# Five extra matmuls into an unread PSUM bank ahead of the first matmul of the feed-forward's context expert

## The reference, cut to what matters

```python
x = x + _layernorm(_L0_attn_ref(_layernorm(x), ...))   # long convolution along the tokens
x = x + _layernorm(_L0_ffn_ref(_layernorm(x), ...))    # 8 routed experts + a shared one
x = x + _layernorm(_L1_attn_ref(_layernorm(x), ...))   # 16 heads, causal, 2 null keys
x = x + _layernorm(_L1_ffn_ref(_layernorm(x), ...))    # 4 unlike experts, top 2 of 4
```

```python
logits = x @ router_w + router_b + load_balancer
e0 = silu(x @ sw_w1) * (x @ sw_w3) @ sw_w2
syn = x @ ce_syn_w + ce_syn_b
attn = (syn @ ce_wv + ce_bv) @ ce_wo + ce_bo
h2 = _layer_norm(syn + attn, ce_n1g, ce_n1b)           # the context expert, e2
```

## Time and profile before

| | us |
|---|---|
| median of 3 runs | 1162.09 |
| lowest, highest | 1157.04, 1163.64 |
| the profiled execution, its own time | 1157.97 |
| its span, first to last instruction | 1156.2 |
| mean granted TensorE clock | 0.962 |

### The profile page before, as it was taken

One profiled execution on the slowest core, in us unless ns is written; L12 is line 12 of the kernel. 1 busy time (PEld: TensorE's weight loads), 2 busy tenths in 40 slices (PEclk: granted clock), 3 DMA queues, 4 the chain that ended last, 5 costly groups with the idle time before them and its releaser, 6 DMA issues.

```text
span 1156.2 us, 18943 instructions
## 1 busy us (share of the span) xinstructions
PE 1017.6 (88%) x6783; PEld 832.9 (72%) x6783; DVE 797.4 (69%) x2569; ACT 561.1 (49%) x1075; POOL 582.1 (50%) x561
## 2 busy tenths in 40 slices
PE   0568799899988999899998999899999999899976
PEld 0446688578965889568886789668886788669844
DVE  7676666868488666887578685886678764883464
ACT  4217542764346542673436633565427743485421
POOL 4226463754537462655627644574627643565422
PEclk9967899999999999999999999999999999999988
DMA  6200000000000000000000000000000000000000
GB/s 153 70 1 1 10 1 1 1 10 2 1 10 1 10 1 10 1 10 1 1 10 1 10 1 1 10 10 1 1 10 1 1 1 10 1 1 2 10 1 9
DMA packets 21853, 11.29 MB, mean 10 GB/s; under 512 B 7424, under 2 KB 21120, under 8 KB 21632
## 3 DMA queue, kind: packets, MB, share of 16 engines
q1 hardware_dynamic: 18048, 8.84, 2.9%
q10 hardware_dynamic: 3712, 1.25, 0.4%
HBM read 7.99 MB, written 2.10 MB: 9 GB/s over the span
## 4 chain that ended last, share of the span: by engine, by line
PE 47%; DVE 31%; POOL 8%; ACT 6%; issue 6%; DMA 0%; SPq 0%; DVEq 0%; POOLq 0%; ACTq 0%
PE bank L1757 9%; PE bank L1533 6%; POOL rnorm L783 4%; PE bank L1759 4%; ACT square L965 3%; PE bank L1657 3%; PE bank L1717 3%; PE bank L1526 3%; PE bank L1829 3%; PE bank L1527 3%; PE bank L1528 3%; DVE x4m L1494 2%; DVE sumsq L1371 2%; PE bank L1787 2%; PE bank L1723 2%
## 5 line engine op out<-in xcount | busy, mean ns | idle before, releaser
L783 POOL TENSOR_TENSOR rnorm<-sumsq,minus_half 128x16 f32<-128x16 f32 x64 | 192.9, 3027 | 27.0 <-DVE sumsq L1374 27.0
L791 POOL TENSOR_TENSOR square<-square,causal 128x256 f32<-128x256 f32 x128 | 91.6, 747 | 100.4 <-ACT square L1003 100.4
L791 POOL TENSOR_TENSOR unit<-unit,causal 128x256 f32<-128x256 f32 x128 | 90.3, 737 | 85.9 <-ACT unit L1003 85.9
L1398 DVE TENSOR_TENSOR denom<-bank,null_sum 128x4 f32<-128x4 f32 x128 | 20.4, 159 | 122.3 <-PE bank L1759 122.2
L1717 PE MATMUL bank<-qT,kT 64*128 64x256 f32 x512 | 96.4, 389 | 0.0
L1371 DVE TENSOR_REDUCE sumsq<-square 128x16 f32<-128x1024 f32 x64 | 77.9, 1217 | 14.5 <-ACT square L965 14.4
L1757 PE MATMUL bank<-val,unit 128*128 128x128 f32 x512 | 82.2, 283 | 4.2 <-DVE mixed L1402 4.2
L958 ACT ACTIVATE unit<-bank 128x512 f32<-128x512 f32 x128 | 72.1, 599 | 28.0 <-PE bank L1528 24.9
L1380 DVE TENSOR_TENSOR unit<-unit,rnorm 128x1024 f32<-128x1024 f32 x64 | 79.0, 1241 | 8.9 <-POOL rnorm L783 7.6
L1757 PE MATMUL bank<-val,square 128*128 128x128 f32 x512 | 82.3, 283 | 2.6 <-DVE mixed L1402 2.6
L1723 PE MATMUL bank<-qT,kT 64*128 64x128 f32 x512 | 84.0, 284 | 0.5 <-ACT unit L1003 0.3
(11 more groups left out here) (360 smaller groups left out, 2782.3 us busy)
## 6 DMA issues: line engine op xcount, KB each, us to landing
out<-x SPq DMA_DIRECT2D x8, 256.0 KB, 2.2
xin<-in_L_attn_x SPq DMA_DIRECT2D x7, 256.0 KB, 2.7
square<-in_L_attn_w_kv SPq DMA_DIRECT2D x1, 1024.0 KB, 7.8
w_sw<-in_L_ffn_sw_w SPq DMA_DIRECT2D x3, 256.0 KB, 8.2
unit<-in_L_attn_w_q SPq DMA_DIRECT2D x1, 512.0 KB, 6.4
w_out<-in_L_attn_w_out SPq DMA_DIRECT2D x1, 512.0 KB, 4.3
w_ml<-in_L_ffn_ml_w SPq DMA_DIRECT2D x2, 256.0 KB, 5.7
xin<-in_L_attn_x ACTq DMA_DIRECT2D x1, 256.0 KB, 3.0
```

The lines of the kernel that those rows point to most:

```text
L783: pool.tensor_tensor(rnorm[:, k, t, :], sumsq[:, t % 2, k, :], minus_half[:], ALU.pow).then_inc(a_root.sem, 1)
L791: m = pool.tensor_tensor(pd, pd, causal[:].unsqueeze(1).to_broadcast([P, 2, P]), ALU.mult)
```

## The change

A new step `f_warm` is played on TensorE. It waits for nothing, and it signals nothing. It issues five matmuls of one fp32r weight slice with 512 columns of the same tile, `w_kv.hi`, into bank 6. `f_ce.0` overwrites part of bank 6 later, and nothing reads what `f_warm` wrote. The step is in three of the tables, so in seven rounds.

```diff
 MIDDLE = { "PE": """
-a_m.0 a_m.1 a_null f_turn.0 f_turn.1 f_ce.0 f_ce.1 f_sw.0 ...
+a_m.0 a_m.1 a_null f_turn.0 f_turn.1 f_warm f_ce.0 f_ce.1 f_sw.0 ...
 LAST_L = { "PE": """
-a_m.0 a_m.1 f_turn.0 f_turn.1 a_null f_ce.0 f_ce.1 f_sw.0 ...
+a_m.0 a_m.1 f_turn.0 f_turn.1 a_null f_warm f_ce.0 f_ce.1 f_sw.0 ...
 LAST_A = { "PE": """
-a_m.0 a_m.1 f_turn.0 f_turn.1 a_null f_ce.0 f_ce.1 f_sw.0 ...
+a_m.0 a_m.1 f_turn.0 f_turn.1 a_null f_warm f_ce.0 f_ce.1 f_sw.0 ...
...
+            def f_warm(g):
+
+                for _ in range(5):
+                    mm(bank[6][:], w_kv.hi[:, 0:P], w_kv.hi[:, 0:N], start=True, stop=True)
...
-                "f_turn": f_turn, "f_ce": f_ce_, "f_sw": f_sw, ...
+                "f_turn": f_turn, "f_warm": f_warm, "f_ce": f_ce_, "f_sw": f_sw, ...
```

More of the change, by code:

```diff
@@ L82 @@
     "PE": """
-a_m.0 a_m.1 a_null f_turn.0 f_turn.1 f_ce.0 f_ce.1 f_sw.0 f_me.0 l_turn2 a_t.0 f_ceT f_sw.1 a_m.2 f_sw.2 f_relu.0 a_v.0 f_relu.1 a_t.1
+a_m.0 a_m.1 a_null f_turn.0 f_turn.1 f_warm f_ce.0 f_ce.1 f_sw.0 f_me.0 l_turn2 a_t.0 f_ceT f_sw.1 a_m.2 f_sw.2 f_relu.0 a_v.0 f_relu.1 a_t.1
 f_ce2 a_m.3 f_sw.3 f_me.1 a_v.1 f_ml.0 f_ml.1 f_ce2T a_t.2 f_ml.2 f_ml.3 a_t.3 l_turn3 a_v.2 a_v.3 l_route f_out.0
@@ L112 @@
     "PE": """
-a_m.0 a_m.1 f_turn.0 f_turn.1 a_null f_ce.0 f_ce.1 f_sw.0 f_me.0 a_t.0 f_sw.1 f_ceT a_m.2 f_relu.0 f_relu.1 a_v.0 f_sw.2 f_ce2 l_turn2
+a_m.0 a_m.1 f_turn.0 f_turn.1 a_null f_warm f_ce.0 f_ce.1 f_sw.0 f_me.0 a_t.0 f_sw.1 f_ceT a_m.2 f_relu.0 f_relu.1 a_v.0 f_sw.2 f_ce2 l_turn2
 a_t.1 a_m.3 f_me.1 f_sw.3 a_v.1 a_t.2 f_ce2T f_ml.0 f_ml.1 f_ml.2 f_ml.3 a_t.3 a_v.2 a_v.3 f_out.0 l_turn3 f_out.1
@@ L142 @@
     "PE": """
-a_m.0 a_m.1 f_turn.0 f_turn.1 a_null f_ce.0 f_ce.1 f_sw.0 f_me.0 a_t.0 f_sw.1 a_m.2 f_ceT f_sw.2 a_v.0 f_relu.0 f_relu.1 a_t.1 f_ce2
+a_m.0 a_m.1 f_turn.0 f_turn.1 a_null f_warm f_ce.0 f_ce.1 f_sw.0 f_me.0 a_t.0 f_sw.1 a_m.2 f_ceT f_sw.2 a_v.0 f_relu.0 f_relu.1 a_t.1 f_ce2
 a_m.3 f_sw.3 a_v.1 f_me.1 a_t.2 f_ml.0 f_ml.1 f_ml.2 a_t.3 f_ml.3 a_v.2 f_ce2T a_v.3 f_out.0 f_out.1 f_out.2
@@ L1876, in _ @@
                 "a_scores": a_scores, "a_mix": a_mix_, "a_ot": a_oT_, "a_out": a_out_,
-                "f_turn": f_turn, "f_ce": f_ce_, "f_sw": f_sw, "f_me": f_me_, "f_ml": f_ml_,
+                "f_turn": f_turn, "f_warm": f_warm, "f_ce": f_ce_, "f_sw": f_sw, "f_me": f_me_, "f_ml": f_ml_,
                 "f_cet": f_ce_apply, "f_relu": f_relu_, "f_ce2": f_ce2, "f_ce2t": f_ce2_apply, "f_out": f_out,
```

## The result

| | before | after |
|---|---|---|
| median of 20 runs, us | 1161.23 | 1153.54 |
| lowest, highest | 1156.86, 1164.45 | 1149.72, 1157.23 |
| the profiled execution, its span | 1157.97, 1156.2 | 1154.32, 1152.6 |
| its mean granted TensorE clock | 0.962 | 0.976 |

The ratio is 0.9941, with a 95% interval from 0.9928 to 0.9955: 0.59% faster, 5.2 to 8.4 us. The time lies in the predicted range, 3.4 us under the point.

What follows compares the result with a forecast made beforehand. Neither TensorE (47% of the chain) nor VectorE (31%) alone bounds the kernel; the chain passes between them. Cost 0, `f_ce` -3.75 and `f_ml` -1.5 sum to -5.2 us: 1162.1 to 1156.9 us, range 1151 to 1162.

Steps and rivals of the forecast that it cites:

- The five cost nothing: Ahead of `f_ce`: five matmuls take 1.17 us inside an idle stretch of 1.19 to 1.40 us, so cost 0.
- No fall at `f_ce`: At `f_ce`, dense work in the idle stretch keeps the clock at 1.00, so the five falls do not come.
- 0.75 us a fall: At `f_ce`, each avoided fall saves about 0.75 us: 2.25 us in `MIDDLE`, 1.5 in `LAST_L` and `LAST_A`, sum 3.75.
- `f_ml`: At `f_ml`, one to one and a half of five sliding falls should miss, at 1.3 us each: 1.5 us gained.
- The sum, -5.2 us: Whole kernel: 0 - 3.75 - 1.5 = -5.2 us, taking the profiled execution from 1157.97 to 1152.8 us.
- The last step: Whole kernel: the same -5.2 us put on the median, 1162.1 to 1156.9 us, 0.45% less.
- Little is left of it: Rival: falls at `f_ce` vanish, five stay at `f_ml`, new ones come behind `f_me`; gain about 2 us, 1160 us, chance 0.2.
- It doesn't do what it says: Rival: the clock falls at `f_ce` nonetheless, since equal idle stretches come with and without falls; 1162 us, chance 0.1.
- Slower: Rival: the five run at 1.2 GHz and outlast the wait before `f_ce`; 7.7 us lost, 1170 us, chance 0.06 with smaller overruns.

Runs made afterwards that it cites:

- the two kernels with further fills: Changed kernel plus eight matmuls ahead of `f_ml.0` in the five middle rounds, ratio 0.9911; the same with fills in setup, first round and `LAST_F` besides, 0.9897.
- the kernel with both fills: Changed kernel plus eight 512-column matmuls ahead of `f_ml.0` in the five middle rounds; ratio 0.9911 against the kernel before, 1151.7 us.

## Why the prediction was right, point by point

The mechanism was right at `f_ce`, where the change stands. That the sum came so near is partly luck, since three errors at `f_ml` and `f_ce` cancelled.

- *The five cost nothing.* Right. `f_ce` starts 0.43 us after the copy begins in both kernels. The margin was larger than I said: eight, 0.5 us over the stretch, cost at most 0.27 us a round.
- *No fall at `f_ce`.* Right in all seven rounds of both profiles; with the eight and the two kernels with further fills it is none in 35 rounds. Two readings behind it were too wide. The clock was not at 1.00 to the end of the idle stretch in every round: in four of the five rounds it fell 0.12 to 0.43 us before `f_ce` began, which is still 0.8 us or more after `f_warm` would start. And "wherever TensorE does such work" the windows do not always show 1.00: the window of the fifth round in the earlier trace rows has TensorE busy throughout at 0.50, and in the experiment with the five one step later they ran at 0.50 in the third round.
- *0.75 us a fall.* Right, a little low: `f_ce` to power 6.14 to 5.34 us, rounds shorter by 0.7 to 1.0, 4.2 us for the five in place of 3.75. In `LAST_A` 107.70 became 106.70. In `LAST_L` 130.05 became 129.37 in the kernel with both fills; in the changed kernel it grew to 130.73, because a new fall behind `f_me` cost 1.4 us. I had expected such a one in a middle round and at less than 1 us, with the chain on VectorE and GpSimd; here the chain ran over TensorE, where the sixteen transposes behind `f_me.0` took 3.29 us against 1.94 in the kernel with both fills.
- *`f_ml`.* I took one to one and a half falls fewer, at 1.3 us. It was two fewer, at 1.3: 2.6 us in place of 1.5. The price was right, but the 1.85 us that it was taken from were 1.7: I set 1.72 us for the first four of line 1829 at the high clock, which is what a later group takes, and they take 1.98. That these falls are on the path was an inference then; the fill ahead of `f_ml.0` alone shows it. The ground for the count, a fall that slides later until it misses, is not borne out: in the changed kernel line 1829 takes 3.49, 2.90 and 2.92 us in rounds one, two and four, and the rounds between and behind them miss. With eight in place of five only the third round missed. That some would miss was right, how many was luck.
- *The sum, -5.2 us.* The profiles give 5.55 us over the rounds, from other parts: 4.2 at `f_ce` and 2.6 at `f_ml` gained, 1.4 lost to the new fall, which the sum did not have. The two that were too small and the one left out nearly cancel.
- *The last step was the weak one:* I put the profiled execution's difference on the median. The runs differ by 7.7 us in the medians (5.2 to 8.4 by the interval). The kernel before has a mean clock of 0.9605 over its runs and 0.962 in the profiled one, which is one fall more, about 1 us. That the profiled time lay 4.1 us under the median was a sign of it. Of the rest, the changed kernel's profiled execution lies 0.8 us over its own median; all of it is within the interval. So the forecast said "within 0.5%" as likelier, and it came out at 0.59%.
- *The rivals.* "Little is left of it" fell: the new fall took back 1.4 of some 7 us. "It doesn't do what it says" fell too. Its ground remains true and unexplained: in rounds without a filling the same wait comes with a fall and without. The rule of the Trainium skill (TensorE: Matmul & The Clock Gate, "HAM oscillation") gives idle gaps as what lets the clock fall; the trace agrees only in part. The clock fell in 12 of 21 rounds with a gap of 1.2 to 1.4 us, and in two of seven with one of 0.63 to 0.94 us. It fell in two of seven with ten thin matmuls and 0.4 us or less, and once with twelve thin ones and no gap.
- *Slower* fell: all of `f_warm` ran at 1.00.

What stays open: why a given round keeps the clock and its neighbour with the same work does not; whether it is the density of the work or the idle time that decides in this stretch, since thin matmuls without a gap and dense ones with a gap each had one or two falls in a single profile; and what share of the gain in the setup is from the fills and what from its scatter.

## What to carry to other kernels

Where a chain passes through short matmuls behind a short wait, look at the granted clock in that place and not at its mean: five unread matmuls in a wait of 1.3 us gave 0.6%, though the page has TensorE busy for 88% of the span. Put them into the wait, not near it, make them dense, and keep them about as long as the wait. Find the dearest fall first, here the one at `f_ml`: a fill there alone gave 0.7%, part of it by moving the falls near `f_ce`. And a round that gets shorter meets the clock's falls elsewhere: count them in the whole profile, and compare stretches between fixed points, since the setup alone scattered by 5 us.

## What the runs showed of the hardware that was not expected

Thin matmuls keep the clock up in part: ten with 32 columns gave a mean clock of 0.9694, twelve that leave no idle time 0.9697, two with 512 columns 0.9719, five 0.9753, none 0.9605. Dense work that came after the fall had begun did not end it: with the five matmuls behind `f_ce` the low stretch lasted 6.8 us in two rounds, where it lasts 3.4 in the kernel before. And executions of one kernel can have their falls in exactly the same rounds (895.61 and 895.63 us over the seven) while their setups differ by 2 us.
